# State-space output projection: the last five of eight k tiles as three rounded products each, with high parts in buffers that are idle at that time

## What is computed

```python
def mamba2(X, W_in, conv_w, conv_b, dt_bias, A_log, D, norm_w, W_out):
    z, xBC, dt = split(X @ W_in.T)                  # 1024, 1024 + 2 * 64, 16 columns
    dt = softplus(dt + dt_bias)
    x, Bm, Cm = split(silu(conv4(xBC) + conv_b))    # causal convolution of 4 taps
    y = scan(exp(dt * -exp(A_log)), dt * Bm * x, Cm) + D * x
    y = y * silu(z)                                 # 512 tokens x 1024, the tile g
    y = y * rsqrt(mean(y * y) + EPS) * norm_w
    return y @ W_out.T                              # 1024 -> 512, the output projection
```

## Time and profile before

| What | us |
|---|---|
| median of three runs | 2042.44 |
| the profiled execution | 2042.29 |
| its span, first to last instruction | 2040.6 |
| busy TensorE (matmul) | 1908.5 (94%) |
| busy VectorE | 1411.8 (69%) |
| busy ScalarE | 1226.2 (60%) |
| busy GpSimd | 467.1 (23%) |
| matmuls of the output projection, L1127, x512 records | 226.1 |
| mean granted TensorE clock | 0.977 of full |

### The profile page before, as it was taken

One profiled execution on the slowest core, in us unless ns is written; L12 is line 12 of the kernel. 1 busy time (PEld: TensorE's weight loads), 2 busy tenths in 40 slices (PEclk: granted clock), 3 DMA queues, 4 the chain that ended last, 5 costly groups with the idle time before them and its releaser, 6 DMA issues. The chain is left out here.

```text
span 2040.6 us, 38546 instructions
## 1 busy us (share of the span) xinstructions
PE 1908.5 (94%) x12588; PEld 1270.2 (62%) x12588; DVE 1411.8 (69%) x2857; ACT 1226.2 (60%) x3068; POOL 467.1 (23%) x661
## 2 busy tenths in 40 slices
PE   7899999999999998788999999999999999899988
PEld 5667676767676766355565656555666555478853
DVE  8878787878787878446666666657676757565438
ACT  4436363636353534248969696878787877556614
POOL 2212121213121212320322222212222222200006
PEclk9899999999999999888999999999999999999999
DMA  6222222222222132333343433324333332641166
GB/s 212 61 61 82 62 82 62 82 65 78 74 70 82 61 82 62 111 91 92 85 120 89 108 102 89 115 59 125 84 110 88 100 95 70 193 150 62 62 191 263
DMA packets 120045, 200.61 MB, mean 98 GB/s; under 512 B 23088, under 2 KB 44592, under 8 KB 119600
## 3 DMA queue, kind: packets, MB, share of 16 engines
q1 hardware_dynamic: 110640, 179.20, 29.1%
q0 software_dynamic: 9216, 18.89, 3.6%
HBM read 117.27 MB, written 29.88 MB: 72 GB/s over the span
## 5 line engine op out<-in xcount | busy, mean ns | idle before, releaser
L1811 ACT ACTIVATE a_shared<-a_shared,a_mx 128x512 f32<-128x512 f32 x512 | 341.4, 670 | 62.3 <-DVE a_mx L1872 62.2
L1804 ACT ACTIVATE a_probs<-a_scores 128x512 f32<-128x512 f32 x512 | 292.2, 604 | 93.2 <-PE a_scores L2016 91.0
L1872 DVE TENSOR_REDUCE a_mx<-a_shared 128x1 f32<-128x512 f32 x512 | 318.9, 682 | 17.8 <-PE a_shared L1998 16.9
L2016 PE MATMUL a_scores<-a_qs,a_ks 98*128 98x512 f32 x512 | 218.9, 435 | 23.6 <-ACT a_probs L1804 19.9
L1998 PE MATMUL a_shared<-a_ks,a_qs 96*128 96x512 f32 x512 | 217.0, 436 | 21.5 <-ACT a_shared L1811 14.7
L1127 PE MATMUL m_outp<-m_wout,m_g 128*128 128x512 f32 x512 | 226.1, 600 | 2.7 <-issue 2.7
L1972 PE MATMUL a_shared<-link 128*128 128x512 f32 x768 | 190.9, 402 | 9.2 <-POOL a_ident L1731 6.3
L676 DVE SCALAR_TENSOR_TENSOR m_acc<-m_proj,m_cw,m_acc 128x511 f32<-128x511 f32 (+2 forms) x216 | 158.8, 747 | 53.5 <-ACT m_acc L492 48.4
L553 ACT ACTIVATE m_xw<-m_added,m_wdt 128x64 f32<-128x64 f32 x256 | 56.0, 330 | 218.5 <-DVE m_xdt L764 218.5
L967 PE MATMUL m_proj<-m_xt_hi,link 128*128 128x512 f32 x448 | 182.1, 407 | 1.0 <-DVE m_acc L676 1.0
L1972 PEld LDWEIGHTS a_shared<-link 128*128 128x128 f32 x768 | 144.6, 192 | 61.0 <-ACT a_shared L1811 12.6
(11 more groups left out here) (279 smaller groups left out, 3679.9 us busy)
## 6 DMA issues: line engine op xcount, KB each, us to landing
m_dec<-step_decay SPq DMA_DIRECT2D x64, 256.0 KB, 4.0
a_qs<-link SPq DMA_DIRECT2D x256, 64.0 KB, 2.3
m_ce<-run_decay SPq DMA_DIRECT2D x128, 112.0 KB, 3.6
a_ks<-a_k_hi POOLq DMA_DIRECT2D x192, 64.0 KB, 2.5
e_x<-x SPq DMA_DIRECT2D x11, 1024.0 KB, 5.4
m_xt_in<-x_t_in SPq DMA_DIRECT2D x8, 1024.0 KB, 7.6
m_x_tok<-x_in SPq DMA_DIRECT2D x8, 1024.0 KB, 6.3
x<-m_x_tok SPq DMA_DIRECT2D x32, 256.0 KB, 2.2
```

Of the source, the lines that this page charges most:

```text
L1804: act.activation(probs[:, n % 2, h, :], scores[t.score_bank(n, h)][:, :], ACT.Exp, scale=-1.0).then_inc(exp_ready, 1)
L1811: act.activation(scored[:, :], scored[:, :], ACT.Exp, scale=-1.0, bias=mx[:, i % 2, j, h:h + 1], accum_out=den[:, i, j, h:h + 1]).then_inc ...
L1872: dve.tensor_reduce(mx[:, i % 2, j, h:h + 1], bank(what)[:, :], AX.X, ALU.min).then_inc(mx_ready, 1)
L2016: pe.matmul(scores[t.score_bank(n, h)][:, :], ks[0:STACK + 2, t.slot(i), h, j * P:(j + 1) * P], qs[0:STACK + 2, t.slot(i), h, :], start=Tr ...
```

## The change

For the k tiles 3 to 7 of the output projection (`WHOLE` = 3, `XT_TILES` = 8) each float32 matmul becomes three of float32r: high of g times high of the weight, high times low, low times high. Tiles 0 to 2 stay as they are.

Once: ScalarE copies the five weight tiles to `wout_hi` (in group 1 of the first sequence), and GpSimd subtracts them from `wout` in place (in group 2).

In each sequence ScalarE copies tiles 3 to 5 of g to high parts (the early ones, behind the squares of tiles 4 and 5 in group 3) and tiles 6 and 7 (the late ones, behind the squares of tiles 6 and 7). VectorE subtracts them from g in place (`over` gives a view at the place of the buffer allocated next, so `wout_low` lies in `wout`, `early_hi` in `xt_in`, `late_hi` in `xdt`, `g_low` in `g`): the early ones in group 3 ahead of `skip_added`, the late ones between `raw_sizes` and `softplus` of the next sequence, where it waits for the late high parts. The high parts lie in `xt_in` (in the last sequence in `xt_lo`) and in `xdt`. The counts of the semaphores `sq_ready` and `g_ready` go from 8 to 10 a sequence; the waits of `silus`, `squares` and GpSimd's sums are renumbered and otherwise as before.

```diff
+WHOLE, LATE = 3, 6
+        wout_low = over("wout_low", XT_TILES)
         wout = sb("wout", [P, XT_TILES, DM])
+        wout_hi = sb("wout_hi", [P, XT_TILES - WHOLE, DM], F32R)
+        early_hi = over("early_hi", KT)
+        late_hi = over("late_hi", XT_TILES - LATE)
+        g_low = over("g_low", XT_TILES)
+        wout_lo, g_lo = wout_low[:, WHOLE:, :], g_low[:, WHOLE:, :]
+        def gate_high(k, more):
+            if k >= LATE:
+                return late_hi[:, k - LATE, :]
+            return early_hi[:, 1 + k - WHOLE, :] if more else xt_lo[:, 1 + k - WHOLE, :]
+        GATED = [n + 1 + (n >= LATE) for n in range(XT_TILES)]
+        def split_at(b, late):
+            return at(b, GATES, GATES if late else LATE + 1)
...
@@ gpsimd, body @@
                     carried_factors(b, first, gr)
+                    if first and gr == 2:
+                        pool.wait_ge(const, SET + 2)
+                        pool.tensor_tensor(wout_lo, wout[:, WHOLE:, :], wout_hi[:, :, :].bitcast(F32), ALU.subtract
+                                           ).then_inc(const, 1)
...
@@ scalar @@
+            def gate_highs(b, late, more):
+                if not late and more:
+                    act.wait_ge(xt_split, at(b, KT, 2 * KT))
+                for k in range(LATE, XT_TILES) if late else range(WHOLE, LATE):
+                    ins = act.activation(gate_high(k, more), g[:, k, :], ACT.Copy)
+                ins.then_inc(sq_ready, 1)
...
                         squares(b, first, gr - 1)
+                    if gr + 1 == NG:
+                        gate_highs(b, False, more)
...
+                    if first and gr == 1:
+                        act.wait_ge(const, SET + 1)
+                        act.activation(wout_hi[:, :, :], wout[:, WHOLE:, :], ACT.Copy).then_inc(const, 1)
...
                 squares(b, first, NG - 1)
+                gate_highs(b, True, more)
                 if more:
                     head(b + 1, False)
...
@@ vector @@
+            def gate_lows(b, late, more):
+                dve.wait_ge(sq_ready, split_at(b, late))
+                for k in range(LATE, XT_TILES) if late else range(WHOLE, LATE):
+                    ins = dve.tensor_tensor(g_lo[:, k - WHOLE, :], g[:, k, :], gate_high(k, more).bitcast(F32),
+                                            ALU.subtract)
+                ins.then_inc(g_ready, 1)
...
                     if gr + 1 == NG and more:
                         conv(b + 1, 8, 1, 1, 1)
+                    if gr + 1 == NG:
+                        gate_lows(b, False, more)
                     skip_added(b, first, gr, 0)
...
                 if more:
                     raw_sizes(b + 1, False)
+                gate_lows(b, True, more)
+                if more:
                     softplus(b + 1)
...
@@ tensor, out_proj @@
-                for k in range(XT_TILES):
-                    ins = pe.matmul(outp[t % 2][:, :], g[:, k, t * P:(t + 1) * P], wout[:, k, :],
-                                    start=(k == 0), stop=(k == XT_TILES - 1))
+                for k in range(WHOLE):
+                    pe.matmul(bank[:, :], g[:, k, tile], wout[:, k, :], start=(k == 0), stop=False)
+                for k in range(WHOLE, XT_TILES):
+                    if t == 0 and k == LATE:
+                        pe.wait_ge(g_ready, split_at(b, True))
+                    high, low, n = gate_high(k, more)[:, tile], g_lo[:, k - WHOLE, tile], k - WHOLE
+                    pe.matmul(bank[:, :], high, wout_hi[:, n, :], start=False, stop=False)
+                    pe.matmul(bank[:, :], high, wout_lo[:, n, :], start=False, stop=False)
+                    ins = pe.matmul(bank[:, :], low, wout_hi[:, n, :], start=False, stop=(k == XT_TILES - 1))
```

More of the change, by code:

```diff
@@ L140, in mamba_stage, with over @@
         pair_sum = sb("pair_sum", [2 * NH, NH])
+        def over(name, tiles):
+            return nc.alloc_sbuf_tensor_at("m_" + name, [P, tiles, SEQ], F32R, offset=-(-nc.sbuf_base // 32) * 32)
+        wout_low = over("wout_low", XT_TILES)
         wout = sb("wout", [P, XT_TILES, DM])
+        wout_hi = sb("wout_hi", [P, XT_TILES - WHOLE, DM], F32R)
         cw = sb("cw", [P, 9, 4])
@@ L270, in mamba_stage, with gated_at @@
         link_lo = sem("link_lo")
+        wout_lo, g_lo = wout_low[:, WHOLE:, :], g_low[:, WHOLE:, :]
[3 more added lines that the diff above has]
+            return early_hi[:, 1 + k - WHOLE, :] if more else xt_lo[:, 1 + k - WHOLE, :]
+        GATES = XT_TILES + 2
+        GATED = [n + 1 + (n >= LATE) for n in range(XT_TILES)]
+        def gated_at(b, n):
+            return at(b, GATES, GATED[n % XT_TILES] + GATES * (n // XT_TILES))
+        def split_at(b, late):
+            return at(b, GATES, GATES if late else LATE + 1)
         N_SMALL = 8
@@ L442, in sum_squares @@
                     if n == 0:
-                        squares = value(pool, at(b, XT_TILES, 1))
+                        squares = value(pool, gated_at(b, 0))
                         met(pool, const, SET)
@@ L449, in sum_squares @@
                     else:
-                        pool.wait_ge(sq_ready, at(b, XT_TILES, n + 1))
+                        pool.wait_ge(sq_ready, gated_at(b, n))
                         pool.wait_ge(sq_used, at(b, XT_TILES, n))
@@ L523, in xc_silus @@
                     if gr >= 2 or not first:
-                        act.wait_ge(g_ready, at(b, XT_TILES, 2 * (gr - 2) + 2))
+                        act.wait_ge(g_ready, gated_at(b, 2 * gr - 3))
                     act.activation(xc[:, gr % 2, j, :], acc[:, j, :], ACT.Silu).then_inc(xc_ready, 1)
@@ L559, in squares @@
                     n = 2 * gr + j
-                    act.wait_ge(g_ready, at(b, XT_TILES, n + 1))
+                    act.wait_ge(g_ready, gated_at(b, n))
                     if n >= 2 or not first:
@@ L1115, in mean_square, with out_proj @@
                 ins.then_inc(rms_done, 1)
-            def out_proj(b, t):
+            def out_proj(b, t, more):
                 if t == 0:
-                    pe.wait_ge(const, SET + 1)
-                    pe.wait_ge(g_ready, at(b, XT_TILES, XT_TILES))
+                    pe.wait_ge(const, SET + 3)
+                    pe.wait_ge(g_ready, gated_at(b, XT_TILES - 1))
                 if t == 0:
@@ L1125, in out_proj @@
                     pe.wait_ge(out_read, at(b, TT, t - 1))
-                for k in range(XT_TILES):
-                    ins = pe.matmul(outp[t % 2][:, :], g[:, k, t * P:(t + 1) * P], wout[:, k, :],
-                                    start=(k == 0), stop=(k == XT_TILES - 1))
+                bank, tile = outp[t % 2], slice(t * P, (t + 1) * P)
+                for k in range(WHOLE):
[7 more added lines that the diff above has]
+                    ins = pe.matmul(bank[:, :], low, wout_hi[:, n, :], start=False, stop=(k == XT_TILES - 1))
                 ins.then_inc(out_done, 1)
@@ L1169, in body @@
                         x_tile(b + 1, False, n)
-                out_proj(b, 0)
+                out_proj(b, 0, more)
                 mean_square(b)
@@ L1177, in body @@
                 for t in range(1, TT):
-                    out_proj(b, t)
+                    out_proj(b, t, more)
             over_overlapped(pe, n_seq, head, body)
```

## The result

The changed kernel took 2057.52 us (median of 4 runs, 2055.3 to 2060.29); the kernel before, on the same chip, 2042.45 (4 runs). The ratio is 1.0067, with a 95% interval of 1.0054 to 1.0079: slower, by 15 us.

What follows compares the result with a forecast made beforehand. TensorE and a chain through other engines end level at each hand-over. Seven hand-overs + 20.3, last sequence - 2.4, first sequence + 1.0, on 2042.3 us gave 2061.2 us, range 2054 to 2069.

Steps and rivals of the forecast that it cites:

- Chain and TensorE level at the end of a hand-over: At `added_states` of group 0, the chain's `weighted_x` ends at 561.60 and TensorE starts at 561.74, so neither has slack.
- Chain + 2.9 us: Hand-over: early low parts 1.8 and late high parts 1.05, with semaphore waits, lengthen the chain by 2.9 us (2.6 to 3.4).
- early high parts: Three ScalarE copies at about 507.3, 1.6 us, covered by the following tap's 2.86 us wait for TensorE: nothing taken.
- late low parts: Two VectorE subtractions ahead of `softplus`, 1.25 us, hidden before Ln at 522.7 even if GpSimd delays their end to 522.2.
- Hand-over + 2.9: Each of the seven hand-overs between sequences gets 2.9 us longer, + 20.3 in sum.
- First wait 3.5: TensorE waits 3.5 us ahead of the first z tile, for VectorE's convolution of the first x tile.
- Second wait 2.9: TensorE waits 2.9 us ahead of `added_states` in group 0, until the chain arrives at 564.5.
- Rival 3: Slow clock: behind the first wait 0 to 0.5 us a hand-over; behind the second 1.7 each, about 2073 us; 15%.
- Rivals 1 and 2: At `added_states` TensorE arrives last, 2015 to 2022 us (5%); or chain idle time absorbs the work, 2039 to 2045 (5%).
- Last sequence - 2.4: No z tiles there, so TensorE's gain of 3.4 us shows, less part of the early low parts: - 2.4 (- 3.5 to 0).
- First sequence + 1: `wout_lo`, 6.9 us of GpSimd beside a pace-setting VectorE, costs 1 us (0 to 3); `wout_hi` on ScalarE costs nothing.
- Later stages 0: Unchanged code behind the last sequence: the forecast's sum has no term for it.

Runs made afterwards that it cites:

- both halves of the change: Two kernels, the changed kernel with only k tiles 3 to 5 split (2060.39 us) or only 6 and 7 (2055.63 us); kernel before 2044.04 us.

## Why the prediction was right, and where its terms were off

The direction, the reason (the added work is on a chain that ends level with TensorE) and the total held: 2061.2 predicted, 2060.3 in the profiled execution, 2057.5 as the median, 3.7 below and inside the range. What TensorE does behind the first wait was wrong, and part of the agreement is luck of the terms.

- **Chain and TensorE level at the end of a hand-over: right.** Less TensorE turned into waits, a shorter chain gained nothing, and both together gained 2.04 us a sequence.
- **Chain + 2.9 us: right**, 2.84 (1.80 early low parts, 1.04 late high parts). The early high parts (1.66 us at 522.03) were covered as said: the tap behind them waited 1.29 for TensorE, where it had waited 2.86. The late low parts took 2.26 us, not 1.25, beside GpSimd's sums, and ended 0.6 us ahead of Ln: hidden, as said.
- **Hand-over + 2.9: mis-sized, 2.35.** Two steps gave 0.5 back: convolution to scan got 0.29 shorter, and scan to `weighted_x` 0.22. The second is the slack that I had not read. I took one hand-over, and it was the one with the shortest way from scan to `weighted_x`, 18.22 us, and the longest from convolution to scan, 15.89; the means are 18.50 and 15.46. In four of the other six VectorE waited in `norm` for TensorE, 1.8 us in sum, about 0.5 each in the three with the shortest way to the scan (15.2). So in these TensorE and not the transfer set the time, and the chain had that much slack. By the query on that line in the kernel before, whose other two waits, 3.4 us, are in the last sequence:

```profile
its engine sat idle before it (us, times) until:
  PE m_outp L1127: 5.2, 6
```

  The 0.29 lies in a round trip through DRAM that varies by more than this from one hand-over to the next, so I don't claim a cause for it.
- **First wait 3.5: right**, 3.17 to 3.25. **Second wait 2.9: wrong**, 0 to 0.83. The slow clock behind the first wait slows TensorE by up to 2.5 us, and so it comes to the second place with the chain or a little ahead of it: the second wait is at most 0.2 us in the three hand-overs with 6.8 us at 0.50, and 0.37 to 0.83 us in the four with 3.4. Rival 3 named this as its harmless part; it was the rule. That the added work alone costs 4.2 to 5.3 a hand-over shows what it would cost without the shorter products.
- **Rival 3** did not happen in the changed kernel at its place, since the second wait had all but gone; it did in both halves of the change and in the kernel without k tile 7. **Rivals 1 and 2** fell.
- **Last sequence - 2.4: mis-sized**, - 1.5, inside its bounds.
- **First sequence + 1: wrong**, + 5.6, outside the bounds of 0 to 3. I priced GpSimd's long subtraction at 6.9 us (6.13 measured) and let it meet "a few instructions only". It met two products that the chain of the first sequence needed, and held them for its whole length; the squares, the convolutions and TensorE (a wait of 3.12 us at 91.76) were late behind them. The products themselves lost 4.6 of the 5.6. The kernels without the subtraction differ by 2.6 us at the first tap among themselves, and the changed one is 3.4 to 6.1 above them, so the rest may be chance. That the two met at all was chance in part, as the transfer ahead of GpSimd's product landed 1.7 us earlier than in the kernel before. The Trainium skill, SBUF — State Buffer, section "Who interferes with whom", says that an instruction of the one engine waits out a whole instruction of the other; this trace agrees (8.36 us beside 6.13, 1.28 alone). I had applied that rule at the hand-over, where it cost nothing, and not here.
- **Later stages 0**: - 2.4 in unchanged code, which takes 1180.8 to 1186.4 us in the traces of the ten kernels. I see no effect of the change in it.

So the profiled execution, the slowest of the four, came within 1.0 us of the sum by terms that cancel: measured less predicted, + 4.6 in the first sequence, - 3.9 in the hand-overs, + 0.9 in the last one, - 0.2 in the groups, - 2.4 in the later stages.

## What to carry to other kernels

Before work moves from a busy engine to others, look where the engines meet: an engine that is 98% busy can still arrive level with a chain, and then only a change that shortens both gains. Take the new work off the chain first (squares and step sizes moved past what waits for them), then split: with three tiles split this was 13 us faster than the kernel before, and 16 slower in the old order. Read every repetition of a meeting point, not one, and put a long one-time instruction of GpSimd where VectorE has slack, not where it sets the pace.

## What the runs showed of the hardware that was not expected

- A slow stretch can hide a wait. A first wait of 3.2 us was followed by 3.4 or 6.8 us at 1.2 GHz, and in place of a second wait of 2.9 us there was one of 0.37 to 0.83 or of at most 0.2. Waits of 2.40 and 2.71 us were followed by windows with a mean of 0.54, while in the new order, with none there, the clock stayed at 1.00 in the hand-overs. The length of the wait alone does not decide: in the kernel without k tile 7 the clock was 0.55 behind a second wait of 2.19 us (window 259.20 to 262.60) and 1.00 behind one of 2.61 (359.10 to 365.90), and with tiles 6 and 7 alone it was 0.57 behind a first wait of only 0.93 (226.74 to 230.14).
- One GpSimd subtraction of 128 x 2560 (6.13 us) held a pair of VectorE products of 1.28 us for 8.36, with the GpSimd product ahead of it; beside that product alone (2.12 us) the pair took 3.00 in the kernel without k tile 7. Four scans beside GpSimd took 5.06 instead of 2.43.
- From the issue of the decays' store to that of their load it took 2.77 us in one kernel and 4.45 in another, at the same place and in the same code, because the second of two stores landed after 3.5 us instead of 1.9. A chain through DRAM carries this spread into the distances.
